# Matrices of ones and zeros made two tiles at a time, by seven comparisons with one number per partition each

## The reference

```python
emb = jax.vmap(lambda tbl, idx: tbl[idx], in_axes=(0, 1), out_axes=1)(embed_tables, sparse)
bi = emb[:, FIRST, :] * emb[:, SECOND, :]          # 325 pairs of fields, 32 numbers each
a = jax.nn.relu(jnp.einsum('bpd,dh->bph', bi, att_w_w) + att_w_b)
scores = jnp.einsum('bph,ho->bpo', a, att_d_w) + att_d_b
att_weight = jax.nn.softmax(scores, axis=1)
att_out = jnp.sum(att_weight * bi, axis=1)
x = jnp.concatenate([att_out, dense], axis=-1)
out = jax.nn.sigmoid(x @ fin_w + fin_b)
```

## Time and profile before

| | |
|---|---|
| median of 3 runs | 463.61 us (463.41 to 464.05) |
| the profiled execution's own time | 461.92 us |
| its span, from the first instruction to the last | 460.1 us |
| busy: PE, DVE, POOL, ACT | 395.4, 394.3, 332.4, 130.2 us |
| TensorE's granted clock, mean of the span | 0.957 of full speed |

### The profile page before, as it was taken

One profiled execution on the slowest core, in us unless ns is written; L12 is line 12 of the kernel. 1 busy time (PEld: TensorE's weight loads), 2 busy tenths in 40 slices (PEclk: granted clock), 3 DMA queues, 4 the chain that ended last, 5 costly groups with the idle time before them and its releaser, 6 DMA issues.

```text
span 460.1 us, 9277 instructions
## 1 busy us (share of the span) xinstructions
PE 395.4 (86%) x2508; PEld 227.7 (49%) x2508; DVE 394.3 (86%) x638; ACT 130.2 (28%) x305; POOL 332.4 (72%) x350
## 2 busy tenths in 40 slices
PE   1596979998999779699999759998999889799884
PEld 1485645543439555345427626554535765434122
DVE  5999897999987678899987678799988687798995
ACT  3203311242452111033263111124253211114353
POOL 5877777777777777777777777777777777777720
PEclk9979989999999899899999988999999979989999
DMA  8557322222213322322213232323221223222210
GB/s 297 92 153 162 28 15 25 17 26 15 14 14 27 26 15 25 15 27 15 15 15 24 16 25 15 26 16 25 16 15 14 16 14 16 13 15 12 18 7 1
DMA packets 16308, 15.44 MB, mean 34 GB/s; under 512 B 7952, under 2 KB 15360, under 8 KB 15872
## 3 DMA queue, kind: packets, MB, share of 16 engines
q0 software_dynamic: 11072, 5.69, 23.7%
q1 hardware_dynamic: 2800, 6.79, 4.2%
q10 hardware_dynamic: 2384, 2.37, 1.9%
HBM read 14.79 MB, written 0.02 MB: 32 GB/s over the span
## 4 chain that ended last, share of the span: by engine, by line
POOL 55%; issue 20%; PE 12%; DVE 9%; DMA 3%; ACT 1%; DVEq 0%; ACTq 0%
POOL emb L436 55%; DVE ring L875 6%; PE first L487 4%; PE sums_f L497 3%; DMA emb<-tables,rows 2%; PE looked_own L470 2%; PE sums_s L511 2%; DVE onehot L775 1%; PE back L470 1%; DVE emb_t L851 1%; PE back L535 1%; DVE look_masked L860 0%; DMA ids<-sparse 0%; POOL emb_placed L425 0%; ACT shared L623 0%
## 5 line engine op out<-in xcount | busy, mean ns | idle before, releaser
L436 POOL DMA_INDIRECT emb<-tables,rows x300 | 283.6, 945 | 91.5 <-issue 90.2
L875 DVE TENSOR_TENSOR ring<-emb_t,turned 128x512 f32<-128x512 f32 (+9 forms) x180 | 191.8, 1100 | 0.3
L470 PE MATMUL looked_own<-look_parts,onehot 128*128 128x448 f32 x546 | 125.0, 381 | 8.1 <-DVE look_masked L860 4.9
L470 PEld LDWEIGHTS looked_own<-look_parts,onehot 128*128 128x128 f32 x546 | 104.2, 195 | 34.4 <-issue 21.3
L487 PE MATMUL first<-ring,par 128*32 128x512 f32 (+1 forms) x672 | 90.1, 609 | 28.6 <-DVE ring L875 28.1
L604 ACT ACTIVATE hidden<-first,par 128x512 f32<-128x512 f32 (+1 forms) x84 | 56.5, 678 | 176.7 <-PE first L487 176.3
L470 PE MATMUL back<-look_parts,onehot 128*128 128x448 f32 x350 | 83.6, 393 | 13.2 <-issue 8.6
L497 PE MATMUL sums_f<-ring,par 128*32 128x512 f32 (+1 forms) x672 | 91.1, 593 | 0.0
L470 PEld LDWEIGHTS back<-look_parts,onehot 128*128 128x128 f32 x350 | 69.4, 203 | 31.0 <-issue 18.0
L851 DVE STREAM_TRANSPOSE emb_t<-emb 128x128 f32<-128x128 f32 x100 | 29.9, 302 | 41.1 <-DMA emb<-tables,rows 33.4
L775 DVE TENSOR_TENSOR onehot<-chunk_of,turned 128x896 fp32r<-128x896 f16 x60 | 63.1, 1052 | 0.1
(11 more groups left out here) (76 smaller groups left out, 128.7 us busy)
## 6 DMA issues: line engine op xcount, KB each, us to landing
emb_placed<-tables SPq DMA_DIRECT2D x768, 0.1 KB
emb<-tables,rows POOLq DMA_INDIRECT x300, 3.4
ring<-tables SPq DMA_DIRECT2D x2, 1568.0 KB, 9.2
shared<-tables SPq DMA_DIRECT2D x1, 1568.0 KB, 8.2
chunk_of<-chunk_numbers ACTq DMA_DIRECT2D x12, 128.0 KB, 3.0
ring<-tables SPq DMA_DIRECT2D x1, 896.0 KB, 5.6
emb<-tables,rows_first POOLq DMA_INDIRECT x44, 4.2
ring<-tables SPq DMA_DIRECT2D x1, 672.0 KB, 6.8
```

Source lines behind the costliest of these rows:

```text
L436: pool.indirect_dma_start(emb[:, f, g * D:(g + 1) * D], None, stacked, bass.IndirectOffsetOnAxis(ap=row, axis=0), element_offset=at,).then ...
L470: mm = nc.tensor.matmul(looked_rows[look_bank[tile]], onehot[:, tile % ONEHOTS, c, :], look_parts[:, n, c, k, :], start=c == 0 and k == 0, ...
L875: nc.vector.tensor_tensor(slot[:, at:at + n, :], emb_t[:, i:i + n, :], turned[f % 2][:, 0, :].unsqueeze(1).broadcast_to((P, n, P)), ALU.mu ...
```

## The change

A pair of tiles (`PAIR = 2`) now has its matrices made together, in seven `tensor_scalar` instructions, one for each chunk. Each compares 256 numbers (two tiles of 128 samples) with one number per partition, which is read from `par` in SBUF. `onehot` has two buffers of two tiles, in place of three of one. The copies of the seven numbers in PSUM are gone. Some small tiles of the start (`clamped`, `look_id` and its like) now lie inside `hidden`, to make room.

```diff
-ONEHOTS = 3
+PAIR = 2
@@
-        onehot = sb("onehot", [P, ONEHOTS, CHUNKS, P], f32r)
+        onehot = sb("onehot", [P, 2, CHUNKS, PAIR * P], f32r)
@@
-        chunk_here = [turned[i][:, 2, 0:CHUNKS] for i in range(2)]
@@ look_up, on PE
-                    pe.wait_ge(onehot_made, tile + 1)
+                    pe.wait_ge(onehot_made, tile // PAIR + 1)
@@ load_chunks, on ACT
-                        act.wait_ge(onehot_made, (block - LOOKS + 1) * G)
+                        act.wait_ge(onehot_made, (block - LOOKS + 1) * G // PAIR)
@@ on DVE
-            def make_onehot(tile, f):
-
-                of, n, g = place_of(tile)
-                numbers, here = chunk_of[:, n, g * P:(g + 1) * P], chunk_here[f % 2]
+            def make_onehots(pair):
+
+                of, n, g = place_of(pair * PAIR)
+                cut = slice(g * P, (g + PAIR) * P)
                 if of == 0 and n == 0:
                     dve.wait_ge(chunk_first_spread, 1)
-                    numbers, here = chunk_first[:, g * P:(g + 1) * P], par[:, cols["look_chunk"]]
+                    numbers = chunk_first[:, cut]
                 elif of == 0:
                     dve.wait_ge(chunk_of_first_in, 16)
+                    numbers = chunk_of[:, n, cut]
                 else:
                     dve.wait_ge(chunk_of_in[n], of * 16)
-                if tile >= ONEHOTS:
-                    dve.wait_ge(looked, tile - ONEHOTS + 1)
-                shape = (P, CHUNKS, P)
-                nc.vector.tensor_tensor(onehot[:, tile % ONEHOTS], numbers.unsqueeze(1).broadcast_to(shape),
-                                        here.unsqueeze(2).broadcast_to(shape), ALU.is_equal).then_inc(onehot_made, 1)
+                    numbers = chunk_of[:, n, cut]
+                if pair >= 2:
+                    dve.wait_ge(looked, (pair - 1) * PAIR)
+                here = par[:, cols["look_chunk"]]
+                for c in range(CHUNKS):
+                    eq = nc.vector.tensor_scalar(onehot[:, pair % 2, c, :], numbers, here[:, c:c + 1], None, ALU.is_equal)
+                eq.then_inc(onehot_made, 1)
@@
-            make_onehot(0, 0)
-            make_onehot(1, 0)
+            make_onehots(0)
             make_low(0, 0)
             make_low(0, 1)
-            make_onehot(2, 0)
+            make_onehots(1)
@@
-            for here in chunk_here:
-                nc.vector.tensor_copy(here, par[:, cols["look_chunk"]]).then_inc(chunk_here_made, 1)
@@
-                        if tile < 2:
-                            make_onehot(3 + tile, 0)
+                        if tile == PAIR - 1:
+                            make_onehots(2)
@@
-                        if tile + 1 < TILES:
-                            make_onehot(tile + 1, f)
+                        if tile % PAIR == PAIR - 1 and tile + 1 < TILES:
+                            make_onehots(tile // PAIR + 1)
@@
-                    make_onehot(end_tile, 0)
+                    make_onehots(end_tile // PAIR)
```

More of the change, by code:

```diff
@@ L187, in attention_fm @@
         ids = sb("ids", [P, T, F], i32)
-        clamped = sb("clamped", [P, T, F])
         rows_first = sb("rows_first", [P, G, FIRST_FIELDS], i32)
@@ L202, in attention_fm @@
         chunk_of = sb("chunk_of", [P, CHUNK_BLOCKS, G * P], CHUNK_DT)
-        look_id = sb("look_id", [P, LOOKS, T])
-        look_part = sb("look_part", [P, LOOKS, T])
-        look_chunk = sb("look_chunk", [P, LOOKS, T])
-        look_i = sb("look_i", [P, LOOKS, T])
         look_mask = sb("look_mask", [P, LOOKS, T, CHUNK_ROWS])
-        onehot = sb("onehot", [P, ONEHOTS, CHUNKS, P], f32r)
+        onehot = sb("onehot", [P, 2, CHUNKS, PAIR * P], f32r)
         look_masked = sb("look_masked", [P, D, CHUNK_ROWS])
@@ L214, in attention_fm @@
         hidden = sb("hidden", [P, HIDDEN, PAIRS_C * P])
+        look_id, look_part, look_chunk, look_i = (hidden[:, HIDDEN - 1, n * LOOKS * T:(n + 1) * LOOKS * T].rearrange(
+            "p (n t) -> p n t", n=LOOKS) for n in range(4))
+        clamped = hidden[:].rearrange("p h e -> p (h e)")[:, 0:T * F].rearrange("p (t f) -> p t f", f=F)
         shared = sb("shared", [P, 2 * PAIRS_C * P + 2 * G * WIDTH])
@@ L298, in attention_fm @@
         chunk_of_in = [sem(f"chunk_of_in{i}") for i in range(CHUNK_BLOCKS)]
-        chunk_here_made = sem("chunk_here_made")
         look_id_steps = sem("look_id_steps")
@@ L469, in look_up @@
                                 pe.wait_ge(made[k], 1 if c == 0 else 2)
-                            mm = nc.tensor.matmul(looked_rows[look_bank[tile]], onehot[:, tile % ONEHOTS, c, :],
+                            mm = nc.tensor.matmul(looked_rows[look_bank[tile]], onehot[:, tile // PAIR % 2, c, tile % PAIR * P:(tile % PAIR + 1) * P],
                                                   look_parts[:, n, c, k, :], start=c == 0 and k == 0,
@@ L819, in _ @@
             rows_of = par[:, cols["look_row"]].unsqueeze(1).broadcast_to((P, LOOKS * T, CHUNK_ROWS))
-            i_of = look_i[:].rearrange("p n t -> p (n t)").unsqueeze(2).broadcast_to((P, LOOKS * T, CHUNK_ROWS))
+            i_of = look_i.rearrange("p n t -> p (n t)").unsqueeze(2).broadcast_to((P, LOOKS * T, CHUNK_ROWS))
             nc.vector.tensor_tensor(look_mask[:].rearrange("p n t i -> p (n t) i"), rows_of, i_of, ALU.is_equal
                                     ).then_inc(look_mask_made, 1)
-            for here in chunk_here:
-                nc.vector.tensor_copy(here, par[:, cols["look_chunk"]]).then_inc(chunk_here_made, 1)
             dve.wait_ge(look_mask_made, 1)
-            dve.wait_ge(chunk_here_made, 2)
             dve.wait_ge(feats_in, 16)
```

## The result

The changed kernel takes 465.30 us (median of 16 runs, 464.25 to 466.42) and the kernel before 464.06 us on the same chips: a ratio of 1.003, 95% interval 1.0021 to 1.0039. It is slower, by 1.2 us where 8.4 us were forecast. The profiled execution has a span of 463.3 us, 3.2 us more than before's. That overstates the change: the profiled execution of before (461.92 us) was faster than all 16 of these runs of it (463.14 to 465.33), while that of the changed kernel (465.14) lies near its median.

A forecast was written before the change was run, and what follows sets the result against it. POOL's stream of gathers was taken as the bound. Gathers held up by comparisons add 8.4 us: 461.92 + 8.4 = 470.3 for the profiled execution, 472.0 us against the runs' median; 8-in-10 range 464 to 483 us.

The forecast's parts named there:

- POOL's stream bounds the kernel: 346 gathers on POOL, 1.25 us each from start to start, set the time; nothing faster on DVE or PE shortens it.
- The length of a series: Seven comparisons for two tiles on DVE: 1.45 or 2.2 us against 1.96 before; 2.2 was taken.
- the double rate: A tensor_scalar element on DVE takes about half a tensor_tensor element's time, 0.52 against 0.98 ns.
- A DVE instruction holds a gather up until it ends, at two points: A gather waits for the DVE instruction in flight 0.12 us after its start, perhaps also near its end; doubles 8.4 to 16.8.
- the single row at 14.87 us: A gather at the start, beside tensor_scalar L793: it should lose 0.05 us and took 0.99.
- The price: Over 30 series, 1.76 gathers each wait 0.16 us on the mean: 0.28 us a series, 8.4 us in all.
- the lower end: Gather delay with the short comparison of 0.21 us, first part only: 1.16 x 0.105 x 30 = 3.7 us.
- The two tiny copies go too: Two copies into PSUM at the start are removed, some 0.2 us of DVE that POOL does not wait for.
- No effect on POOL: Rival: comparisons do not delay gathers and DVE's change lies in its idle time; 463.5 us, chance 0.16.
- Starving: Rival: each series holds one gather for half its length, 1.1 us x 30 = 33 us; 497 us, chance 0.07.
- the single rate: Rival: comparisons run without the double rate, each series costs DVE 1.2 us more, POOL undisturbed; 468 us, chance 0.11.
- the gain: Rival: DVE's saving counts in the tail and PE waits less for matrices; 461 us, chance 0.06.

The follow-up runs named there:

- after_small: The changed kernel with the look_parts differences cut into pieces of 224 elements: 459.46 us, 0.9909 of the kernel before.
- tt_all: The changed kernel with tiles still paired, but every matrix made by tensor_tensor and the two tiny PSUM copies back: 463.89 us, 0.9996 of the kernel before.
- long_scalar: The changed kernel plus one tensor_scalar of 1792 elements ahead of 12 of the series: 474.35 us, one execution, no ratio.
- mid_scalar: The changed kernel plus one tensor_scalar of 448 or 896 elements ahead of each of 28 series: 469.81 us, one execution, no ratio.
- constant: The changed kernel comparing with constants instead of numbers from par for 30 pairs (looks up wrong rows): 466.90 us, 1.0077 of the kernel before.
- before_shift: The kernel before with its two tiny PSUM copies moved from ahead of the second table's differences to behind them: 464.88 us, 1.0032 of the kernel before.
- tt_rest: The changed kernel with all but the first two pairs made by tensor_tensor and the two tiny PSUM copies back: 463.17 us, 0.9983 of the kernel before.
- before_small: The kernel before with the look_parts differences cut into pieces of 224 elements: 458.40 us, 0.9884 of the kernel before.

## Why the prediction was wrong

*POOL's stream bounds the kernel.* Right in the main. In each of the sixteen traces the last gather starts 434.3 to 434.4 us after the first instruction, plus what all gathers together lose over 0.94 us (5.9 us before, 8.9 us in the changed kernel, 2.0 us in after_small), and removing losses gave 1.2%. But the end does not follow the last gather at a fixed distance. It is 19.9 us in the trace of before, 20.2 in the changed kernel's and up to 22.3 in others (22.1 in tt_all). Differences of 1 us between two traces' ends are therefore not all POOL's, and what sets this last part was not tried.

*The length of a series.* 2.2 us forecast, 2.18 measured at 404.94, and the double rate held for this input and output. The 2.2 is in part luck. The fixed part of 0.18 us came from L834, beside which a gather started; in the eight traces where none did, the same instruction takes 0.23 us, with the next 0.14 us after it, not 0.19. Comparisons start 0.26 us apart, not 0.31, which makes 1.84 us for seven, and the rest is DVE waiting for gathers, a term that the sum does not have. The number per partition costs 0.06 us (0.26 against 0.20 us apart), not 0.1.

*A DVE instruction holds a gather up until it ends, at two points.* Right as a mechanism for an instruction of 448 elements and more; long_scalar and mid_scalar measured what the single row at 14.87 us had suggested, and settled the question that no row showed, whether the gather's second part can be held up as well: it can, by a `tensor_scalar`. The rule as I wrote it, "in flight 0.12 us after its start", is too wide. A gather of the kernel before says so already:

```profile
10.18 0.94 POOL L436 DMA_INDIRECT emb<-tables,rows_first  x1 [0.30 <-issue]
```

The first difference starts at 10.26 and is in flight at 10.30, and the gather lost nothing.

*The price: "Each finds a comparison in flight and waits on the mean half of 0.31", 8.4 us in all.* This is the step that failed. Measured are 0.8 us at most for the 68 gathers concerned. Half a duration would be right if gathers met the comparisons at any place by chance, and had nothing to spare. Both are wrong. A gather can spare 0.12 us, and a comparison that starts just ahead of it, or after it, does not hold it up. And the meeting places are not by chance, since POOL also holds DVE up: I had read that in L813 at 17.05 and gave it no price. It is the larger half of the exclusion here, 8 us of waiting on DVE's side in 51 comparisons, which DVE largely has to spare. In `constant`, where the places are worse, the loss is 3.1 us. That this is close to the 3.7 us of the lower end is chance: 34 gathers lose about 0.09 us each, not every gather half of 0.21.

*"The two tiny copies go too, some 0.2 us at the start, where DVE is not what POOL waits for."* Wrong, and it is where most of the measured 1.2 us comes from. POOL does wait for DVE there, at the ends of the differences, and the copies decided on which side of a gather the second table's difference falls. The rows had shown it: the prediction used the gathers held up by differences as its evidence, and did not ask what the change does to their phase. before_shift, which has no series, is as much slower by that alone (1.0032 against 1.003).

*The rivals.* "No effect on POOL" was nearest in its number, and for the series it nearly holds; the loss at the start it does not have. Starving was not seen in the changed kernel, nor was the single rate or the gain.

What stays open: whether the series cost up to 1 us of their own, what sets the time from the last gather to the end, and the profiled executions' share of luck in the first table's phase, which moves with the arrival of its transfer (that gather lost 0.73, 1.35, 1.84 and 1.48 us in the traces of before, changed, tt_rest and before_shift).

## What to carry to other kernels

Where a stream of gathers sets the end, look for the DVE instructions that it waits behind, and cut the long ones with two SBUF inputs into short pieces; here, with pieces that start 0.30 us apart, that was worth 5 us, where by the prediction's estimate nothing done to the matrices could give more than 0.6. Price an exclusion by where the two sides meet and by what each has to spare, not by half of an instruction's duration: two streams that exclude each other fall into step, and the one that waits may be the one that can afford it. And when 0.2 us is taken away far from the critical path, ask what fixed-phase collision it moves; an undo that carries a second edit along (the copies, here) will blame the wrong one.

## What was not expected of the hardware

A shorter series of comparisons made the kernel slower (1.0077 against 1.003), at least in part since its comparisons met the gathers at a worse place.

A gather can be passed over many times. In the profiled execution of before_small one gather beside a train of 14 pieces, 0.30 us apart, waited for the whole rest of the train:

```profile
11.66 4.32 DVE L783 TENSOR_TENSOR look_parts<-ring,look_parts 128x224 fp32r<-128x224 f32 x14 [2.02 <-ACT look_parts L586]
12.74 1.04 POOL L436 DMA_INDIRECT emb<-tables,rows_first  x1 [0.30 <-issue]
14.09 2.71 POOL L436 DMA_INDIRECT emb<-tables,rows_first  x1 [0.31 <-issue]
```

It starts at 14.09 and ends at 16.80, 0.82 us after the train's end (15.98). That execution took 461.57 us, the six others 457.47 to 458.56. The gathers beside the other small trains got through with 0.2 us lost at most. What decides between the two was not tried.
